# Narrow-head attention: late keys zeroed by GpSimd after the exponentials, and small transposes moved to other PSUM banks

## The reference

```python
scores = einsum('bhqd,bhkd->bhqk', q, k) * hd ** -0.5
scores = where(tril(ones((256, 256))), scores, -inf)   # key later than query: out
attn = softmax(scores, axis=-1)
o = einsum('bhqk,bhkd->bhqd', attn, v)
```

## Time and profile before

| | us |
|---|---|
| median of 3 runs (lowest, highest) | 2002.69 (1999.13, 2006.82) |
| the profiled execution's own time | 2013.94 |
| its span in the trace | 2012.6 |
| PE, DVE, ACT, POOL busy | 1847.9, 1291.7, 1082.4, 602.5 |
| first to last exponential, stage b | 310.76 to 402.10 |
| first to last exponential, stage d | 616.44 to 816.89 |
| first to last exponential, stage f | 1713.89 to 1812.29 |

### The profile page before, as it was taken

One profiled execution on the slowest core, in us unless ns is written; L12 is line 12 of the kernel. 1 busy time (PEld: TensorE's weight loads), 2 busy tenths in 40 slices (PEclk: granted clock), 3 DMA queues, 4 the chain that ended last, 5 costly groups with the idle time before them and its releaser, 6 DMA issues.

```text
span 2012.6 us, 42781 instructions
## 1 busy us (share of the span) xinstructions
PE 1847.9 (92%) x16191; PEld 1542.0 (77%) x16191; DVE 1291.7 (64%) x3373; ACT 1082.4 (54%) x2729; POOL 602.5 (30%) x543
## 2 busy tenths in 40 slices
PE   7999988969998999799999999999999997897995
PEld 6988976646666777589999999999999986674663
DVE  5676655742236555468888888888888886774222
ACT  5666653312223323368888887888888873331221
POOL 5633320032224200333344444433344430003221
PEclk8999999979998999899999999999999997997998
DMA  4000019122238000000000000000000002302222
GB/s 160 20 1 1 1 47 361 53 89 40 46 72 241 2 2 2 21 11 12 11 12 11 27 12 11 11 11 12 11 11 1 1 1 95 167 3 77 40 46 65
DMA packets 51864, 91.75 MB, mean 46 GB/s; under 512 B 4592, under 2 KB 43632, under 8 KB 49232
## 3 DMA queue, kind: packets, MB, share of 16 engines
q1 hardware_dynamic: 42928, 78.16, 11.6%
q0 software_dynamic: 8160, 10.29, 3.3%
q10 hardware_dynamic: 576, 0.56, 0.1%
HBM read 56.13 MB, written 32.87 MB: 44 GB/s over the span
## 4 chain that ended last, share of the span: by engine, by line
PE 71%; DVE 17%; issue 4%; ACT 3%; POOL 2%; DMA 2%; SPq 0%; ACTq 0%; DVEq 0%; POOLq 0%
PE bank L100 59%; PE bank L2353 9%; DVE e_st L2506 1%; DVE a_t L646 1%; DVE d_nm L1313 1%; DVE e_PT_lo L2525 1%; PE bank L1727 1%; POOL c_rows L1607 1%; POOL g_rows L1607 1%; DVE tiny L125 1%; DVE a_t L643 1%; DVE d_nm L1312 1%; DVE f_nm L1313 1%; DVE b_nm L1313 1%; PE bank L446 1%
## 5 line engine op out<-in xcount | busy, mean ns | idle before, releaser
L2506 DVE TENSOR_REDUCE e_st<-bank 128x1 f32<-128x401 f32 x512 | 291.3, 569 | 143.8 <-PE bank L100 136.1
L2443 ACT ACTIVATE e_P<-bank,e_st 128x400 f32<-128x400 f32 (+1 forms) x512 | 307.1, 600 | 105.4 <-DVE e_st L2510 104.6
L2525 DVE TENSOR_TENSOR e_PT_lo<-bank,e_PT_hi 128x512 fp32r<-128x512 f32 (+1 forms) x448 | 287.8, 642 | 0.0
L2353 PE MATMUL bank<-ident,e_P 128*128 128x128 f32 (+1 forms) x1664 | 261.6, 277 | 15.3 <-DVE e_PT_lo L2525 5.0
L2458 ACT CAST e_PT_hi<-bank 128x512 fp32r<-128x512 f32 (+1 forms) x448 | 248.2, 554 | 26.5 <-PE bank L2353 12.1
L100 PE MATMUL bank<-e_PT_hi,e_kv 128*128 128x256 f32 (+1 forms) x832 | 251.1, 322 | 0.0
L2353 PEld LDWEIGHTS bank<-ident,e_P 128*128 128x128 f32 (+1 forms) x1664 | 197.4, 142 | 51.9 <-issue 36.4
L100 PE MATMUL bank<-e_PT_lo,e_kv 128*128 128x256 f32 (+1 forms) x832 | 217.5, 281 | 0.0
L100 PE MATMUL bank<-e_KT,e_qk_hi 128*128 128x402 f32 x512 | 195.0, 381 | 10.0 <-ACT e_P L2443 6.5
L100 PE MATMUL bank<-e_KT,e_qk_lo 128*128 128x402 f32 x512 | 177.5, 347 | 0.0
L100 PEld LDWEIGHTS bank<-e_PT_lo,e_kv 128*128 128x128 f32 (+1 forms) x832 | 159.9, 192 | 0.0
(11 more groups left out here) (448 smaller groups left out, 4943.1 us busy)
## 6 DMA issues: line engine op xcount, KB each, us to landing
c_wall<-in_c_w SPq DMA_DIRECT2D x8, 1536.0 KB, 18.9
g_wall<-in_g_w SPq DMA_DIRECT2D x8, 1536.0 KB, 19.7
c_rows<-normed SPq DMA_DIRECT2D x9, 1040.0 KB, 12.1
g_rows<-normed SPq DMA_DIRECT2D x9, 1040.0 KB, 12.9
e_stage<-in_e_w SPq DMA_DIRECT2D x16, 416.0 KB, 3.2
c_xs<-c_rows SPq DMA_DIRECT2D x23, 130.0 KB, 2.1
g_xs<-g_rows SPq DMA_DIRECT2D x23, 130.0 KB, 2.0
landing<-in_a_wo SPq DMA_DIRECT2D x2, 1024.0 KB, 6.2
```

The source lines that it names most:

```text
L2353: last = pe.transpose(o[0:rows, c * SEQ + i * P:c * SEQ + (i + 1) * P], p[:, i, k0:k0 + rows], ident[:])
L2443: act.activation(Pm[u % 2][:, i, j * PIECE:j * PIECE + n], bank[score_bank[j]][:, 0:n], ACT.Exp, bias=s[:, i, 4:5], accum_out=s[:, i, j:j ...
L2506: last = dve.tensor_reduce(s[:, i, j:j + 1], bank[score_bank[j]][:, 0:PIECE + 1], AX.X, ALU.max)
L2525: dve.tensor_tensor(lo, bank[tb_bank[at % 2]][0:rows, 0:n * SEQ].rearrange("p (c n) -> p c n", c=n), hi.bitcast(F32), ALU.subtract).then_i ...
```

## The change

- The key-major mask matmuls are gone (`mask_keys`; eight a unit). The first matmul into each B bank now opens it.
- After each unit's exponentials GpSimd sets the entries of late keys to zero with two `affine_select` (`select`; 3 x 2 x 128 and 2 x 128 fp32 in each partition, so 1024 elements), and `values` waits for that instead of the exponentials.
- `turn_maxima` writes to bank 5 (B_BANK + 2) once the exponentials of this step have left it, not to bank 7, and stands after `values`; only unit 1 of stage d still uses bank 7. In b and f, `turn_maxima(1)` comes behind the side work of step 0. Work in bank 7 no longer waits for `lower_queries`.
- Transposes of normed rows go to bank 4 (TURN_BANK), wait for the exponentials and not for maxima, and it is now the scores, not `mask_queries`, that wait until they are taken.
- On VectorE the lower half of an entering transpose comes before `normalise`.
- In stage d eight warming matmuls stand in each of steps -1 and 0. GpSimd's work for stage e is cut into parts, one a step behind that step's select; two of the upper copies of it move to steps 8 and 12.

```diff
+                TURN_BANK = B_BANK + 1
                 if U == 4:
-                    BESIDE = [[("k", 1, SIDE)], [("turn", -2, 0), ("v", 1, SIDE)], [("out", -1, SIDE)], [("q", 2, SIDE)]]
+                    BESIDE = [[("k", 1, SIDE)], [("turn", -2, TURN_BANK), ("v", 1, SIDE)], [("out", -1, SIDE)], [("q", 2, SIDE)]]
                     PARTS = [[(-2, 2), (-2, 3)], [], [], [(-1, 0), (-1, 1)]]
                 else:
                     BESIDE = [[], [], [("out", -1, SIDE)], [("q", 1, SIDE)], [("k", 1, SIDE)], [("v", 1, SIDE)],
-                              [("turn", -1, 0)], []]
+                              [("turn", -1, TURN_BANK)], []]
                     PARTS = [[], [], [], [(-1, 0), (-1, 1)], [(-1, 2), (-1, 3)], [], [], []]
...
-                        return [(carried[i - 1], 0)] if 1 <= i <= len(carried) else []
-                    return [(2, 0)] if i == 2 else [(3, 0)] if i == 6 else []
+                        return [(carried[i - 1], TURN_BANK)] if 1 <= i <= len(carried) else []
+                    return [(2, TURN_BANK)] if i == 2 else [(3, TURN_BANK)] if i == 6 else []
+                def turned(n):
+                    return SIDE if U == 8 and n == 1 else B_BANK + 2
...
-                    def turn_maxima(n):
-                        for x in beside(n - 2) if n >= 1 else beside(FIRST):
+                    def side_emptied(i):
+                        for x in beside(i):
                             if x[2] == SIDE:
                                 side_taken(*x)
+                    def turn_maxima(n):
                         pe.wait_ge(*maxed.at(n + 1))
+                        if turned(n) == SIDE:
+                            side_emptied(FIRST)
+                        elif n >= 1:
+                            pe.wait_ge(*exped.at(n))
                         for i in range(2):
-                            last = pe.transpose(bank[SIDE][:, i * P:(i + 1) * P], NM[n % PER][:, i, :], ident[:])
+                            last = pe.transpose(bank[turned(n)][:, i * P:(i + 1) * P], NM[n % PER][:, i, :], ident[:])
                         last.then_inc(*nm_turned.up())
 
-                    def masked(k):
+                    def mask_queries():
 
                         for block in (0, 2):
                             for j in range(4):
                                 at, col = place(block, j)
-                                yield bank[k + at][:, col * P:(col + 1) * P], block == 0 and j < 3
-
-                    def mask_queries():
-                        for o, first in masked(A_BANK):
-                            mm(o, ident_b[:], causal, first, False)
-
-                    def mask_keys():
-                        for o, first in masked(B_BANK):
-                            mm(o, causal, ident_b[:], first, False)
+                                mm(bank[A_BANK + at][:, col * P:(col + 1) * P], ident_b[:], causal, block == 0 and j < 3, False)
...
-                        return mm(o, k if keys_first else q, q if keys_first else k, False, True)
+                        return mm(o, k if keys_first else q, q if keys_first else k, keys_first and j == 3, True)
 
                     def scores(n0, n1):
 
@@ -1098,6 +1104,10 @@
                             pe.wait_ge(*k_kept.at(PER * b + x + 1))
                         if n1 is not None:
                             pe.wait_ge(*lowered.at(n1 + 1))
+                            if n1 == 0:
+                                pe.wait_ge(*v_kept.at(1))
+                            else:
+                                pe.wait_ge(*exped.at(n1))
...
-                        pe.wait_ge(*exped.at(n + 1))
+                        pe.wait_ge(*selected.at(n + 1))
...
                             if n0 >= 1:
                                 pe.wait_ge(*maxed.at(n0))
-                            for x in beside(i - 1) if i > FIRST else []:
-                                if x[2] == A_BANK:
+                            mask_queries()
+                        if i == FIRST:
+                            warm(spare[1], B_BANK + 2)
+                        if n1 is not None:
+                            for x in beside(i - 1):
+                                if x[2] == TURN_BANK:
                                     side_taken(*x)
                             for b, k in enter_turns(i - 1):
                                 pe.wait_ge(xt_lo, turns_in + b + 1)
-                            mask_queries()
-                        if i == FIRST:
-                            warm(spare[1], B_BANK + 2)
                         if n0 is not None or n1 is not None:
                             scores(n0, n1)
                         if i == FIRST:
                             warm(9, B_BANK + 2)
-                        if 0 <= i + 1 < N:
-                            turn_maxima(i + 1)
                         if 0 <= i - 1 < N:
                             values(i - 1)
-                        if 0 <= i + 1 < N:
-                            if i >= 0:
-                                pe.wait_ge(*exped.at(i + 1))
-                            else:
-                                pe.wait_ge(*v_kept.at(1))
-                            mask_keys()
+                        if 0 <= i + 1 < N and (i != 0 or U == 8):
+                            turn_maxima(i + 1)
                         if i == FIRST:
                             continue
-                        if i + 2 < N and (enter_turns(i) or any(x[2] == A_BANK for x in beside(i))):
-                            pe.wait_ge(*maxed.at(i + 3))
+                        if U == 8 and i <= 0:
+                            pe.wait_ge(*k_kept.at(PER))
+                            warm(8, B_BANK + 1 if i < 0 else OUT_BANK)
+                        if i >= 0 and enter_turns(i):
+                            pe.wait_ge(*exped.at(i + 1))
                         for b, k in enter_turns(i):
                             if entering:
                                 enter_tensor(b, k)
                             else:
                                 norm_tensor(turns_in + b, b, k)
+                        side_emptied(i - 1)
                         for x in beside(i):
-                            if x[2] == SIDE and i + 1 < N:
-                                pe.wait_ge(*lowered.at(i + 2))
+                            if x[2] == TURN_BANK:
+                                pe.wait_ge(*exped.at(min(i, N - 1) + 1))
                             if routing and x[0] == "turn" and i == N:
                                 routing.logits(0)
                             side(*x)
+                        if i == 0 and U == 4:
+                            turn_maxima(1)
...
-                        dve.tensor_tensor(q, q, bank[SIDE][:, 0:SEQ], ALU.add).then_inc(*lowered.up())
+                        dve.tensor_tensor(q, q, bank[turned(n)][:, 0:SEQ], ALU.add).then_inc(*lowered.up())
...
+                    def select(n):
+                        p = PT[n % 2]
+                        pool.wait_ge(*exped.at(n + 1))
+                        for blocks, pattern in ((p[:, :, 0:3:2, :], [[0, 3], [0, 2], [1, P]]), (p[:, 0:3:2, 3, :], [[0, 2], [1, P]])):
+                            last = pool.affine_select(blocks, blocks, pattern=pattern, compare_op=ALU.is_ge, fill=0.0, base=0,
+                                                      channel_multiplier=-1)
+                        last.then_inc(*selected.up())
...
+                    if ahead:
+                        ahead.gpsimd_first()
+                    for i in range(N):
+                        select(i)
+                        if routing and i == 1:
+                            routing.gate_gpsimd()
+                        if ahead:
+                            ahead.gpsimd_beside(i)
                     if routing:
-                        routing.gate_gpsimd()
                         routing.scatter(0)
                     if ahead:
-                        ahead.gpsimd_early()
+                        ahead.gpsimd_last()
...
-            KEPT_BESIDE = {3: 0, 4: 1, 7: 2, 10: 3}
+            KEPT_BESIDE = {3: 0, 4: 1, 8: 2, 12: 3}
...
+            ROPED_BESIDE = {0: (1, 0), 1: (1, 1), 2: (1, 2), 5: (2, 0), 6: (2, 1), 7: (2, 2), 9: (3, 0), 10: (3, 1), 11: (3, 2)}
+            LOWERED_BESIDE = {3: 0, 4: 1, 8: 2, 12: 3}
+            def gpsimd_first(self):
+                for part in range(3):
+                    self.rope_context(0, part)
+            def gpsimd_beside(self, i):
+                if i in self.ROPED_BESIDE:
+                    self.rope_context(*self.ROPED_BESIDE[i])
+                if i in self.LOWERED_BESIDE:
+                    self.lower_kv(self.LOWERED_BESIDE[i])
```

More of the change, by code:

```diff
@@ L919, in beside @@
                     if U == 4 and i == N:
-                        last = [("turn", BATCH - 2, 0)]
+                        last = [("turn", BATCH - 2, TURN_BANK)]
                     return [(kind, b + d, k) for kind, d, k in BESIDE[u]
@@ L1380, in vector @@
```

(48 more changed lines are left out.)

2 lines of the change are left out of this document (1 added, 1 removed).

## The result

Over the runs made together the kernel went from 2001.68 us (1999.13 to 2006.82) to 1974.55 (1971.65 to 1976.41): ratio 0.986, 95% interval 0.9835 to 0.9885, a gain of 27.1 us where 32.2 were forecast. The profiled execution took 1976.27 us.

What follows compares the result with a forecast made beforehand. It took the chain of waits to set the step, TensorE standing for VectorE's lowered queries. Terms 10.5 + 6.3 + 2.7 + 9.1 + 4.5 + 5.7 - 6.6 gave 32.2 us off the 2002.69 median: 1970 us, range 1957 to 1991.

Steps and rivals of the forecast that it cites:

- the plain step: Plain loop step of d: 5.14 us against 5.45, VectorE no longer waited for; 35 such steps at 0.30 gain 10.5 us.
- the starts: Starts of b, f and d: projection runs under the maxima; gains 3.0, 1.9 and 1.4, together 6.3 us.
- the transposes: Steps with a transpose in f, b, d: it runs under VectorE's work, only scores behind it; gain 9.1 us.
- d's first steps: Norms of three batches bound the loop; each transpose leaves VectorE's chain, 30.65 us becoming 24.5 to 26; gain 4.5.
- the k steps: Two steps of d projecting k: k starts earlier, under VectorE's work; gains 3.4 and 2.3, together 5.7 us.
- the open ends: Last select of each stage lies open, 3 x 1.9 = 5.7; late VectorE work in b and f 0.9: -6.6 us.
- rival 4: TensorE stands longer in steps with a transpose and its clock falls: gain 15, 1988 us; chance 0.08.
- step 0 of b and f: Side piece, about 0.56 and 1.5 us long, goes under the exponentials, besides 0.3 each: gain 2.7 us.
- The ring: Chain of waits in a plain step: exponentials, turned maxima, side piece, masks and scores, 5.14 us in all.
- Bare steps: Steps with nothing beside them: 4.48 us, with the exponentials waited for instead of VectorE.
- Costly selects (2, 3): Selects at 3.1 to 4.8 us: gain about 20, chance 0.09; over 4.9: all 32 given back, chance 0.05.
- Waits that only move (5): TensorE waits as long for VectorE's backlog as before for lowered queries: gain under 8, about 1998 us; chance 0.05.

Runs made afterwards that it cites:

- the runs side by side: Kernel after, rotations moved, last transpose moved too, and eight warming matmuls more, all beside before at 2009.47 us: 1982.57, 1975.17, 1965.99 and 1970.75 us.
- the first pair: Stage d's rotations moved off steps with layer-norm pieces, against the kernel after (1974.55 us): 1962.88 us, ratio 0.9812 to before.
- the probe: Idle two-input GpSimd product behind the selects of steps 12 and 20, on the kernel with moved rotations: 1978.23 us, those steps 10.88 and 9.93.

## Why the prediction was nearly right, point by point

The total held (1974.55 for 1970, within 1957 to 1991), and so did the mechanism of the plain step, the starts and the transposes. That the total came so close is in part luck: the plain steps gave 7.9 us more than forecast, while d's first steps, the k steps and the open ends with the late steps gave 12.1 less. The signs named ahead were mixed too: plain steps are 4.85 apart and not 5.1 to 5.2, and the clock in d, 0.92, is below the 0.95 that was to speak for rival 4. All terms are read from the starts of the exponentials in the two profiles; a late step is one of the last two of a stage.

| term | forecast | measured |
|---|---|---|
| plain steps (35 in the forecast; here the 40 that are in no other row) | 10.5 | 18.4 |
| starts of the stages | 6.3 | 6.65 |
| step 0 of b and f | 2.7 | 1.45 |
| steps with a transpose | 9.1 | 9.1 |
| first steps of d | 4.5 | 0.0 |
| k steps of d | 5.7 | 0.5 |
| open ends and late steps | -6.6 | -9.0 |
| sum | 32.2 | 27.1 |

- **The plain step.** The ring was right, its sizes not: steps with a 0.44 side piece gained 0.6 for 0.31, since the piece is shorter than the row I took. Steps with a projection gained 0.6 as well; the prediction had them at about 6.0, and the sum priced them at 0.30 all the same. In all, 31 of the 40 gained 0.5 to 0.8. Bare steps stayed at 4.75 (before 4.73), where 4.48 was forecast: the prediction had the exponentials as their limit, and the chain has the maxima.
- **Starts and transposes.** Right in sum; in b the two transposes gained 1.8 for 2.55, in f the first 3.0 for 2.9. A transpose of f, the chain: turned rows, upper half, lower half, and only then the reciprocal that had stood ahead in the earlier trace rows:

```profile
1699.52 0.45 PE bank L193 x4
...
1700.43 0.48 ACT XT_hi L227
1700.93 0.88 DVE XT_lo L233 x2
1701.80 1.68 DVE f_inv L1340
```

- **The step that failed** is the one that priced the rotations behind the select: "the rotations in d come to at most 2.1 a step behind the select, 3.9 of 5.1 us, so the next select isn't late". That sum is right, and asks only whether GpSimd itself is late. It put what VectorE loses meanwhile at nothing, though the trace of before had the row for it in stage a (0.16 us of work in 1.15). In steps 1 and 12 GpSimd's products met norm pieces, VectorE stood up to 1.9 us for each met instruction, and the 4.5 us forecast for d's first steps came to 0.0, the 5.7 for the k steps to 0.5. In step 1 of d, VectorE and GpSimd:

```profile
611.80 1.88 DVE L127 SCALAR_TENSOR_TENSOR tiny<-tiny 128x2 f32<-128x2 f32 x1
...
611.73 1.94 POOL L2233 TENSOR_TENSOR e_roped<-landing 128x832 f32<-128x832 f32 x1
```

With the rotations moved the first four steps of d take 26.1 us for 30.65, which is the 4.5 forecast, and the two k steps 7.67 each, a gain of 4.1 of the 5.7. Of the other 1.6, 1.4 is the selects' own hold, 0.70 a step. (The prediction gives this step as 6.6, 6.8 and 6.9 us: it ends near 701.9, 6.6 after its start, but the gain of 3.4 in the sum means 6.9.) The whole kernel gained 7.4 us by the move in the runs side by side, and 11 by the first pair; the probe gave the loss again, in its two steps, without any rotation. A part of it goes by way of the clock: in the first 34 us of d, after and then with the rotations moved:

```profile
604.00:638.00 34.00, 26.72 (x416) 19.66 (x412) 30.92 (x87) 10.67 (x11) 14.24 (x16) 0.85 0.87 252
```

```profile
602.00:636.00 34.00, 28.08 (x518) 20.68 (x510) 30.75 (x90) 13.63 (x15) 12.29 (x14) 1.00 0.83 242
```

TensorE stood longer for the late maxima and was granted 0.85 and not 1.00 of 2.4 GHz, and did 416 matmuls for 518. That is rival 4's mechanism, in d alone; how much of the 7 to 11 us it is wasn't separated from the waits that caused it.

- **The selects and the late steps.** The selects take 1.23 together for the 1.8 taken. The ends cost 2.25 and not 5.7: 1.2 in b and 1.3 in f, and nothing in d. Late steps of b and f cost 3.1 where I had 0.9, and those of d 3.6 where I had nothing: the new wait of the scores on a transpose is real, and in d it comes with the low clock. The figures that the prediction takes from the Trainium skill for loops with a compare and a select stand in section 7 of "GPSIMD Engine Reference", not in 3.1. The 1.23 lies within the estimate of 0.9 to 1.7 us made from them; at its lower end the prediction's own sum would have been 2.7 better, and not 0.3.
- **The rivals.** Costly selects (2, 3) fell with the 1.23 us and with unchanged plain steps in the kernel without them. The clock (4) holds in d, by way of the collisions and the late steps. Waits that only move (5) hold for the late steps and the bare ones, not for the other plain ones.

What stays open: single steps of d differ by 1 to 1.5 us between two runs of the same code. With the last transpose moved, the first k step is 8.67 and 7.69 us at a granted clock of 0.86 and 1.00, and step 2 is 7.43 and 8.90 at 1.00 and 0.73. So the difference goes with the clock, but no run told why it falls in one execution and not in the other.

## What to carry to other kernels

When work goes to an idle engine, or is only cut and re-timed there, ask beside its own duration what the neighbours execute during it: a hidden GpSimd instruction can hold up a 0.16 us one on VectorE for its whole length. Place GpSimd work that reads SBUF beside VectorE work that reads PSUM, and look at the maxima of small VectorE instructions in the trace, not their means; do so over the whole trace of the kernel before, where the row may already stand in another stage. And remove from a ring of waits first the wait that orders it: the change without the move of the masks gave 23 us here, the removed matmuls only 0.45 us a step, and only once they stood on the path.

## What the runs showed of the hardware

- GpSimd instructions that read SBUF (with two inputs of 128 x 832, 1.57 to 1.94 us) held VectorE instructions of 128 x 2 with two SBUF inputs until their end, 1.5 to 1.9 us for 0.16; a memset of the same size (0.79 us) didn't. In each such pair the GpSimd instruction had begun first. The trace agrees with the Trainium skill, "SBUF — State Buffer", section "SBUF: two separate sides", by which VectorE and GpSimd share one pair of ports as an exclusive lock, taken for a whole instruction, and a VectorE operation with two SBUF inputs is shut out by a GpSimd one that reads SBUF.
- The selects hold VectorE too: L123, with two SBUF inputs, took 0.78 us for 0.16 beside the first select in step 3 of f. Instructions with one tensor input also waited (L145, 0.17 to 0.72 us, and L163, 0.41 to 0.96, beside selects; L142, 0.17 to 0.99, beside a product); why these wait isn't told by these runs.
- VectorE instructions that read PSUM weren't held: beside GpSimd work in the three loops, the last maxima (L1327) took 0.42 us at most, as alone, and the addition to the queries (L1334, one input from PSUM and one from SBUF) 0.42, as alone.
- `affine_select` on 128 x 768 took 874 ns and on 128 x 256 407, so 0.91 ns for each element of a partition and 0.17 us fixed: the rate of the memset in the earlier trace rows, not of a two-input product.
